# ScalarE's share of the masks moved from groups 8, 12, 16 to groups 7, 11, 15, and the watch two groups late in place of three

## The reference, cut to what matters

```
h = max(layernorm(x), 0)
# the only relation present is type 1, with the "loop" weights
p = h @ W_loop.T
v = (p + b_loop) * sigmoid(p @ Wg_loop.T + bg_loop)
s = transpose(adj == 1) @ v
x = x + max(s, 0)
```

## Time and profile before

| | |
|---|---|
| median of 3 runs (lowest, highest) | 103.35 us (103.3, 103.67) |
| the profiled execution's own time | 103.4 us |
| its span, first to last instruction | 101.6 us |
| PE busy | 95.9 us, 94% |
| DVE busy | 90.4 us, 89% |
| ACT busy | 90.9 us, 89% |
| POOL busy | 83.9 us, 83% |
| granted TensorE clock, mean | full |

### The profile page before, as it was taken

One profiled execution on the slowest core, in us unless ns is written; L12 is line 12 of the kernel. 1 busy time (PEld: TensorE's weight loads), 2 busy tenths in 40 slices (PEclk: granted clock), 3 DMA queues, 4 the chain that ended last, 5 costly groups with the idle time before them and its releaser, 6 DMA issues.

```text
span 101.6 us, 2495 instructions
## 1 busy us (share of the span) xinstructions
PE 95.9 (94%) x802; PEld 92.0 (91%) x802; DVE 90.4 (89%) x197; ACT 90.9 (89%) x148; POOL 83.9 (83%) x158
## 2 busy tenths in 40 slices
PE   5998898999999999999999999999999999999960
PEld 2677788999999999999999999999999999999950
DVE  2279999999999999999999999999999789787771
ACT  5059899989999999999899989999899989999990
POOL 2274999999999999999999999999999999990000
PEclk9999999999999999999999999999999999999999
DMA  1899999999999999999999999997997150706346
GB/s 55 255 318 292 291 290 290 293 290 285 289 308 270 297 330 326 311 306 313 291 329 322 286 325 333 326 289 234 279 333 218 41 165 11 208 0 206 103 138 171
DMA packets 50289, 25.45 MB, mean 250 GB/s; under 512 B 867, under 2 KB 50277, under 8 KB 50277
## 3 DMA queue, kind: packets, MB, share of 16 engines
q1 hardware_dynamic: 50000, 25.17, 89.2%
q10 hardware_dynamic: 276, 0.13, 0.5%
HBM read 16.91 MB, written 8.39 MB: 249 GB/s over the span
## 4 chain that ended last, share of the span: by engine, by line
PE 87%; ACT 8%; issue 1%; DVE 1%; ACTq 0%
PE psum L824 26%; PE psum L802 15%; PE psum L807 14%; PE psum L803 14%; PE psum L789 12%; ACT psum L432 3%; ACT junk L464 2%; PE psum L751 2%; PE psum L763 2%; ACT hT_hi L425 2%; ACT xn L444 2%; PE psum L770 1%; PE psum L759 1%; ACT gate L458 0%; DVE zeros L535 0%
## 5 line engine op out<-in xcount | busy, mean ns | idle before, releaser
L365 POOL TENSOR_SCALAR xn<-x_all,mean_neg,rstd 128x128 f32<-128x128 f32 x96 | 42.8, 464 | 0.5 <-issue 0.3
L802 PE MATMUL psum<-w_hi,hT_hi 128*128 128x256 f32 x128 | 33.8, 299 | 1.1 <-ACT hT_hi L425 0.7
L432 ACT ACTIVATE psum<-bias_all 128x1024 f32<-128x1024 f32 x32 | 32.9, 1028 | 2.1 <-DVE vals L583 1.9
L824 PE MATMUL psum<-vals,mask 128*128 128x128 f32 x256 | 33.7, 275 | 0.0
L824 PEld LDWEIGHTS psum<-vals,mask 128*128 128x128 f32 x256 | 31.0, 191 | 0.1
L803 PE MATMUL psum<-w_lo,hT_hi 128*128 128x256 f32 x128 | 31.1, 278 | 0.0
L551 DVE BATCH_NORM_STATS2 stats<-x_all 128x6 f32<-128x256 f32 x64 | 23.9, 418 | 3.1 <-DMA x_all<-in_x 3.1
L802 PEld LDWEIGHTS psum<-w_hi,hT_hi 128*128 128x128 f32 x128 | 24.1, 188 | 2.1 <-issue 1.2
L583 DVE TENSOR_TENSOR vals<-psum,gate 128x512 f32<-128x512 f32 (+1 forms) x33 | 21.9, 664 | 3.4 <-ACT gate L458 2.8
L347 POOL TENSOR_TENSOR rstd<-var_eps,minus_half 128x16 f32<-128x16 f32 (+2 forms) x11 | 24.4, 2217 | 0.1
L803 PEld LDWEIGHTS psum<-w_lo,hT_hi 128*128 128x128 f32 x128 | 24.1, 189 | 0.0
(11 more groups left out here) (38 smaller groups left out, 34.8 us busy)
## 6 DMA issues: line engine op xcount, KB each, us to landing
adj_all<-in_adj SPq DMA_DIRECT2D x16, 512.0 KB, 7.0
x_all<-in_x SPq DMA_DIRECT2D x15, 512.0 KB, 7.0
out<-x_all SPq DMA_DIRECT2D x14, 512.0 KB, 6.1
out<-x_all SPq DMA_DIRECT2D x3, 256.0 KB, 2.3
x_all<-in_x SPq DMA_DIRECT2D x2, 256.0 KB, 3.0
out<-x_all ACTq DMA_DIRECT2D x1, 128.0 KB, 2.5
out<-x_all SPq DMA_DIRECT2D x1, 128.0 KB, 2.5
w_raw<-in_L_gnn_W_loop SPq DMA_DIRECT2D x1, 64.0 KB, 2.4
```

Source lines behind the costliest of these rows:

```text
L365: pool.tensor_scalar(xn[:, g % XN, j * D:j * D + D], x_all[:, g * GC + j * D:g * GC + j * D + D], mean_neg[:, b % BATCH_SLOTS, k:k + 1], r ...
L432: nc.scalar.activation(prod_ps[s].rearrange("p g a d -> p g (a d)"), bias_all[:, :, :].rearrange("p a d -> p (a d)").unsqueeze(1) .to_broa ...
L802: nc.tensor.matmul(to, hi, w_hi[:, :], start=False, stop=False, skip_group_check=True)
L824: last = nc.tensor.matmul(to[:, j * D:j * D + D], mask[:, g % MASKS, j * N:j * N + N], vals[:, s, j * D:j * D + D], start=True, stop=True)
```

## The change

ACT makes masks 0 to 3 in both. Before, it also made those of groups 4, 8, 12, 16, 20 and 24; now those of 7, 11, 15, 19, 23 and 27. POOL makes the other 22 in both. The watch of chunk c stood in round 2c + 3 and stands in round 2c + 2; the one of chunk 14 that was written out behind the last round's work is now made by the loop, at the same place.

```
-    WATCH_LAG = 3
+    WATCH_LAG = 2
...
         def mask_by_act(g):
-            return g < 4 or g % MASKS == 0 and g < LAST_MASK_ACT
+            return g < 4 or g % MASKS == MASKS - 1 and g < LAST_MASK_ACT
...
                 if live(t + 2) and mask_by_act(t + 2):
                     edges(t + 2)
-                if t == GROUPS - 2:
-                    watch(CHUNKS - 2)
```

## The result

The changed kernel takes 104.01 us, against 103.31 us for the kernel before in the same comparison: ratio 1.0063, 95% interval 1.0041 to 1.0085. It is slower by 0.7 us, where I had forecast 103.05 us, 0.3 faster. The profiled execution took 103.82 us with a span of 102.0 us, and the granted TensorE clock was full. A second set of runs gave 1.0070 (1.0041 to 1.0099). Two of the 22 runs of the changed kernel were in a slower state, and all ratios here leave such runs out.

A forecast was written before the change was run, and what follows sets the result against it. PE bounds the kernel (94% busy), with a DVE and ACT cycle pacing its middle; 0.48 - 0.1 - 0.1 = 0.28 us off the profiled 103.4 gives 103.1, median 103.05; range 102.85 to 103.3, 8 in 10 102.5 to 103.65.

The forecast's parts named there:

- the gain: Middle rounds: moving the watch takes the four-round cycle from 10.91 to 10.79 us; four cycles gain 0.48.
- the xn: POOL, first group of each batch: xn stand no later, but POOL's 10.91 could become the pace; 0.1 us off, bounds 0 and 0.25.
- the end: Last rounds: PE's own order sets them and the watches of chunks 14 and 15 stay; counted as 0.
- may give way: POOL's cycle: part of its 10.91 us is contention, so it might shrink rather than hold PE back.
- ACT's 5.34: Middle rounds: the two rounds behind a watch cost ACT 5.34 us wherever it stands, counted from vals to vals.
- DVE's 2.86 in round 13: DVE's own need in that round, 49.01 to 51.87, part of its 5.33 us for two rounds from t = 12.
- It is paid once: Seeds of even rounds, products(15) and the like: about 0.1 us too late, one time only; bounds 0 and 0.6.
- a 5.1: Before the change, products(15) follow some 5.1 us behind vals(12), a distance that holds the 0.14 of round 13's stall.
- 4.92: The distance in us that PE kept behind vals(15) before the change: 59.5 less 54.58.
- The port (rival 4): DVE's xn meet POOL's in the cycle's second half, costing 0.22 to 0.26 us; cycle 11.0, time 104.05; chance 0.12.
- the other masks: Mask 8 and its like come behind POOL's three xn, masks 7, 11, 15 earlier; hidden, with 1.3 us to spare.
- the sign against me: Weight loads of turn_rows(22) or (26) waiting for L365 would show the forecast wrong on POOL.

The follow-up runs named there:

- e1: The kernel before, with POOL made to wait for its own power instruction's result before the mask in each batch: 103.23 us against 103.35.
- e8: The changed kernel with the watch of chunk 13 put back in round 29: 103.77 us, ratio 1.0038 to the kernel before.
- e12: The kernel before with only the watch of chunk 13 moved from round 29 to round 28: ratio 1.0049.
- e9: The changed kernel with mask 4 on ACT, a mask ahead of each batch's first xn, and chunk 13's watch in round 29: 103.50 us against 103.39 before.
- e16: The kernel before with POOL's mask casts 384 columns wide in place of 512: ratio 1.0035.
- e2: The changed kernel with mask 4 given back to ACT: 104.03 us, ratio 1.0060 to the kernel before.
- e7: The changed kernel with POOL's mask casts 384 columns wide in place of 512: 104.18 us, ratio 1.0080 to the kernel before.
- e4: The kernel before with only the watch moved to even rounds, masks left as before: 105.46 us, ratio 1.0213.
- e15: e9 with POOL's mask casts 384 columns wide in place of 512: ratio 1.0101 to the kernel before.

## Why the prediction was wrong

From 0.3 us faster to 0.7 slower is a miss of 1.0. Three terms of the sum make up some 0.9 of it: the gain (0.48), the xn (0.2 beyond the 0.1 taken) and the end (0.2).

**"The xn ... stand no later on POOL than before" (I took 0.1 off, bounds 0 and 0.25): this step failed.** I had counted instructions, not what covers a wait. A mask between the power instruction and the xn hid 0.22 us, and the change took it away in six batches. That POOL "may give way" was true of the kernel before (10.91 with meetings, 10.82 in e1), but behind the change its own row is 10.97 and gives no way. The measured worth of putting the mask back in front is 0.3 us of the time, which is also above the bound of 0.25.

**"The end ... I count 0" failed too.** I had looked at the watches of chunks 14 and 15, which stay, and not at that of chunk 13. It costs 0.2 to 0.3 us in the changed kernel (e8), and 0.5 us in the kernel before, where the watch of the round ahead adds to it (e12).

**The gain of 0.48 was not there: this is the largest term that failed.** Of the sum for the cycle, ACT's 5.34 for the two rounds behind a watch was right where DVE meets nothing: 5.35 in e9 from rounds 12 and 16. In the changed kernel these stretches took 5.49 and 5.52 by DVE's vals, since they hold the long xn. The other half was mis-sized. I took DVE's 2.86 in round 13 as its own work, and some 0.1 of that was a meeting with POOL (2.75 in e1 in round 17). Without meetings the cycle of the kernel before is 5.35 and 5.49 (e1: 10.84 by DVE's vals), and that of the changed order 5.35 and 5.49 (e9). They are equal: the watch in even rounds neither wins nor costs in the cycle. In the kernel before the meeting fell outside the 5.34 and added 0.07 to the cycle in the end; e1 and e16 show that a shift of POOL can remove that, and the change's did not.

With the mask in front again, the changed order does run rounds 12 to 24 in 32.47 to 32.56, against 32.75 before. But its rounds 1 to 12 take 30.36 to 30.54, against 30.11 to 30.27 in the three traces with the instructions of before, and no time is shorter.

**"It is paid once" (0.1, for the seed of even rounds) does not hold in the traces.** In e9 the aggregates from 7 to 8, 11 to 12, 15 to 16 and 23 to 24 are 2.79, 2.76, 2.81 and 2.77 apart in place of 2.69, where the kernel before, behind round 6, stalls only at 12 to 13, 16 to 17, 20 to 21 and 24 to 25, by 0.14 to 0.16. The working there also set a 5.1 from the chain beside a 4.92 from the timeline, though the two views give the start of the same product 0.15 to 0.25 apart; on the timeline alone (51.33 and 59.51 for these products) the shortfall is about 0.15. That the stalls of e9 are waits for the seed is not shown: they are too short for the list of waits.

**The port (rival 4) was the right fear at the wrong place and size.** I had it in rounds 14 and 15 with 0.22 to 0.26; it came in rounds 13, 17 and 21 with 0.29 to 0.33. The rule of the Trainium skill's page "SBUF — State Buffer", section "SBUF: two separate sides", that the shared pair is locked for a whole instruction, agrees with the trace in that an xn which meets a cast ends only behind it, 0.08 in round 17. By full blocking the xn's own 0.34 would have to follow the cast, and 0.08 did; what the rest of the xn did meanwhile no run here shows. I had let the milder rows of before outweigh the rule.

**Right:** the other masks are hidden (no wait for a mask shows in the changed kernel); PE waits for L365 at the first group of a batch, which I had named as the sign against me.

**Open:** how much of the cost of the uncovered wait is the wait, and how much the meetings of DVE's xn with POOL's row that come with it. It can reach the time through PE's own waits for xn or through DVE's longer xn. e2 has none of the first and is as slow, which speaks for the port, and e1, with half of the wait and without the long xn, lost nothing. But e7, which should have freed both, had other losses. Why rounds 1 to 12 are slower in every kernel with the new order is open too.

## What to carry to other kernels

Before an instruction is moved out of a gap, look at what it hides there: the instruction ahead may have a result that the next one must wait for, and the trace of before often has the bare wait somewhere, in brackets, in a row that seems not to matter. Where the last rounds leave out a part of the work, all that feeds the next part is due sooner there; check them by themselves. And when several engines are within one or two per cent of each other, compare undisturbed lengths of the same instruction (here 0.34 of 0.67) before calling a length the engine's own work.

## What was not expected of the hardware

- A dependent instruction on POOL starts 0.17 us behind the end of the power instruction; a waiting cast 0.06 behind it (e1), and one that needs nothing 0.05 ahead of it.
- A DVE xn of 0.34 us takes up to 0.99 when it meets POOL's casts and xn (0.93 in the changed kernel, 0.99 in e4), and POOL's xn 0.585 in place of 0.447 the other way.
- Narrower casts on POOL (0.51 in place of 0.61) made a kernel slower by up to 1% (e15 against e9). In e15's trace the meetings of DVE's xn with POOL moved with them; in e16 the cause is not known.
